# A conditional residual layer: the loads of SyncE's queue stand in line, and the first mask factors are split off

## The chip, the cores and the metric

One core of one Trainium2 chip. The metric is the device time of one execution, in microseconds (us); the lower the better. The kernel before took 590.72 us in the median of three runs (590.47 to 591.55).

## The reference

```python
x = x + _L0_cond_ref(x, cond_8, weight, mask, bias)       # x: 128 batches of 128 x 512

masked_w = weight * mask[None, :, :]                      # 8 groups of 512 outputs x 512 inputs
w_bot = jnp.einsum('bg,got->bot', y, masked_w)            # y = cond_8, 128 x 8
return jnp.einsum('bnt,bot->bno', x, w_bot) + bias
```

For each batch b, eight weight matrices are mixed with the eight numbers of y, the mixture is masked, and the batch's 128 x 512 tile of x is multiplied by it; bias and x itself are added. All in fp32.

## The kernel before, in words

The outputs are cut into two slices of 256, the batches into four windows of 32: eight units, slice by slice. A unit has 16 groups of two batches. A unit's mixed weights are made in 16 bursts of TensorE matmuls, each on 16 outputs (L567, `burst`), which land in PSUM as four tiles of a bank each. Two of the four are brought into `wbot` by VectorE, multiplied by the mask on the way (L469, with `factor_sb`), two by ScalarE as plain copies (L388); for these the mask was put on the weights beforehand, by VectorE for the first pair of chunks and by GpSimd for the others (L284, `multiply_mask`, which waits for the load of the weights and for the load of the mask). The weights `wm` of slice 0 are loaded at the start and those of slice 1 during the fourth unit, over those that are done with.

The jobs are the matmuls of x against the mixed weights. In unit 0 the first eight groups are done in halves as the weights arrive. In the others most groups are done whole (L594, `piece`), one after another, and the rest in rounds of four jobs (L613, `turn`) between which the next unit's bursts are put: such a stage takes four turns. The eight PSUM banks are shared by bursts and jobs in the order in which they come free (`share_banks`), so a burst or a turn can wait for an eviction on VectorE.

The output tile `staged` has six buffers of 512 columns. For output tile m SyncE loads x into it (`load_xn`, L334), VectorE adds the bias (L490), then the sums (L503, from PSUM or from the copy `late_sb` that ScalarE makes), and ScalarE's queue stores it (L393). VectorE's work is in program order: while it waits in L490 for a load of `xn`, the evictions behind it wait too. In a stage of whole groups the bias of tile m+1 is added right after the sums of tile m; in a stage of turns the biases stand between the evictions of the bursts.

SyncE issues nearly all loads, in the order of its program: at the start the weights and masks of a pair of chunks, two of x, one of xn, and so on; then, for each group n from 10 on, the xn that are due (up to four tiles ahead), and x of group n (512 KB, L326) into the buffer of group n-10, for which it waits until that group's last job is done. In the fourth unit, behind eight of these groups, stand a load of weights (512 KB) and one of mask (256 KB), and one of factors (512 KB): that is slice 1. Nothing limits how many loads are under way at once, but the buffers: a load waits when its buffer is in use. ScalarE's queue issues the first mask, y, the first half of the factors, the bias and all stores.

Of the kernel before, what the change touches and what calls it, by code (L numbers as in the profile page):

```python
# [34 lines left out]
OUTB = 6  # L35
# [82 lines left out]
ENDING = JOBS_OF[OUT_TILES - 1]  # L118

X_LEAD = 4  # L120


BANK_OF, TAKEN_FROM = {}, {}
# [74 lines left out]
def cond_resid_kernel(nc: bass.Bass, x, xn, w, mask, factor, bias, yblk, out):  # L198
# [5 lines left out]
    with ctx:  # L204
# [3 lines left out]
        def sem(name):  # L208
            return ctx.enter_context(nc.semaphore(name))
# [23 lines left out]
        s_w = [sem(f"s_w{i}") for i in range(CS)]  # L233
        s_mask = [sem(f"s_mask{i}") for i in range(PAIRS)]
        s_factor = [sem(f"s_factor{i}") for i in range(2)]
        s_mul_v = sem("s_mul_v")
        s_mul_p = sem("s_mul_p")
        s_x = [sem(f"s_x{i}") for i in range(XRING)]
# [63 lines left out]
        def stored(eng, m):  # L302

            eng.wait_ge(s_out[m % OUTB], 16 * (m // OUTB + 1))

        @block.sync
        def _(eng):
            def load_blocks(s, at, count):
                eng.dma_start(wm[:, at:at + count, :], w[s, :, at:at + count, :]).then_inc(s_w[at], 16)  # L309

            def load_mask(s, q):
                eng.dma_start(mask_sb[:, :] if s else first_mask[:, q, :], mask[s, q]).then_inc(s_mask[q], 16)  # L312

            def load_factor(s, half):
                at = slice(half * HALF, (half + 1) * HALF) if s == 0 else slice(0, CS)
                eng.dma_start(factor_sb[:, at, :], factor[s, :, at, :]).then_inc(s_factor[half], 16)  # L316

            def load_x(n):
                if n >= XRING:
                    eng.wait_ge(s_s2, LAST_JOB[X_ORDER[n - XRING]] + 1)  # L320
                elif n >= XRING - PAIRS // GB:
                    q = (n - XRING) * GB + PAIRS
                    masked(eng, 0, q)
                    masked(eng, 0, q + 1)
                u, g = X_ORDER[n]
                eng.dma_start(xs[:, n % XRING, :, :, :], x[u % WINDOWS * GROUPS + g]).then_inc(s_x[n % XRING], 16)  # L326

            def load_xn(m):

                if m == 0:  # L330
                    eng.wait_ge(s_s1, 1)
                elif m >= OUTB:
                    stored(eng, m - OUTB)
                eng.dma_start(staged_of(m), xn[m]).then_inc(s_xn[m % OUTB], 16)  # L334

            load_blocks(0, 0, 1)
            load_blocks(0, 1, 1)
            for q in range(1, PAIRS // 2):
                load_mask(0, q)
                load_blocks(0, 2 * q, 1)  # L340
                load_blocks(0, 2 * q + 1, 1)
            load_x(0)
            load_x(1)
            load_xn(0)
            n = 2
            for q in range(PAIRS // 2, PAIRS):
                load_mask(0, q)
                load_blocks(0, 2 * q, 2)
                if q == PAIRS // 2:
                    load_factor(0, 1)  # L350
                for n in range(n, n + (2 if q < PAIRS - 2 else 1)):
                    load_x(n)
                n += 1
                load_xn(q - PAIRS // 2 + 1)
            load_x(n)
            load_xn(OUTB - 1)
            load_x(n + 1)
            ahead = OUTB
            for n in range(XRING, STEPS):

                end = TILE_OF[LAST_JOB[X_ORDER[n - XRING]]] + X_LEAD + 1
                for m in range(ahead, end):
                    load_xn(m)
                ahead = max(ahead, end)
                load_x(n)
                if n in LOAD_W_AT:
                    q = LOAD_W_AT[n]
                    eng.wait_ge(s_s1, ((WINDOWS - 1) * CS + 2 * q + 2) * TILES)
                    load_blocks(1, 2 * q, 2)
                    if q:  # L370
                        masked(eng, 1, q - 1)
                    load_mask(1, q)
                if n == LOAD_FACTOR_AT:
                    b = WINDOWS * CS - 1
                    for j in range(TILES):
                        if on_vector(b, j):
                            tile_evicted(eng, b, j, GROUPS)
                    load_factor(1, 0)
            for m in range(ahead, OUT_TILES):
                load_xn(m)  # L380

        @block.scalar
        def _(eng):
            def evict(behind):
                for b, j, first, end in parts_of(behind):
                    if not on_vector(b, j):
                        tile_ready(eng, b, j)
                        eng.activation(tile_place(b, j, first, end), tile_sums(b, j, first, end),  # L388
                                       ACT.Copy).then_inc(s_ev_a, 1)

            def store_out(m):
                eng.wait_ge(s_o, JOBS_BY[m])
                eng.dma_start(out[m], staged_of(m)).then_inc(s_out[m % OUTB], 16)  # L393

            def load_y(u):
                if u >= 2:
                    eng.wait_ge(s_s1, (u - 1) * CS * TILES)
                eng.dma_start(y_sb[:, u % 2, :], yblk[u % WINDOWS]).then_inc(s_y[u % 2], 16)

            def store_last():  # L400
                for i in ENDING:
                    eng.wait_ge(s_o, i + 1)
                    at = STARTS[i] % BANK
                    eng.dma_start(out[OUT_TILES - 1, :, at:at + WIDTH[i]],
                                  staged_job(i)).then_inc(s_out[(OUT_TILES - 1) % OUTB], 16)

            eng.dma_start(first_mask[:, 0, :], mask[0, 0]).then_inc(s_mask[0], 16)  # L407
            load_y(0)
            eng.dma_start(factor_sb[:, 0:HALF, :], factor[0, :, 0:HALF, :]).then_inc(s_factor[0], 16)
            for b in range(HALF):  # L410
                evict(b)
                if b == HALF - 4:
                    eng.dma_start(bias_sb[:, :], bass.AP(tensor=bias.tensor, offset=bias.offset,
                                                         ap=[[0, P], [1, NO]])).then_inc(s_bias, 16)
            kept = made = 0

            def store_made():
                for m in range(kept, made):
                    store_out(m)
                return made  # L420

            def take_out(jobs):
                for i in jobs:
                    if i in LATE[2:]:
                        eng.wait_ge(s_o, LATE[LATE.index(i) - 2] + 1)
                    eng.wait_ge(s_s2, i + 1)
                    eng.activation(late_of(i), ps[BANK_OF[i, None]][:, 0:SL], ACT.Copy).then_inc(s_late, 1)  # L427

            for stage in STAGES:
                if stage.jobs[0] in NEXT_Y:  # L430
                    load_y(NEXT_Y[stage.jobs[0]])
                if stage.around:
                    for n in range(TILES + 1):
                        if n == TILES:
                            take_out(stage.jobs[2:])
                        for b in stage.bursts_at(n):
                            evict(b)
                            kept = store_made()
                else:
                    for b in stage.bursts:  # L440
                        evict(b)
                        kept = store_made()
                if made - kept >= 2:
                    kept = store_made()
                end = stage.jobs[-1]
                made = min((STARTS[end] + WIDTH[end]) // BANK, OUT_TILES - 1)
            kept = store_made()
            store_last()
            for i in range(OUTB):
                count = len(range(i, OUT_TILES, OUTB)) + (len(ENDING) - 1 if i == (OUT_TILES - 1) % OUTB else 0)  # L450
                eng.wait_ge(s_out[i], 16 * count)
# [8 lines left out]
        def _(eng):  # L460
            def evict(behind):
                for b, j, first, end in parts_of(behind):
                    if on_vector(b, j):
                        tile_ready(eng, b, j)
                        if b in (0, HALF):
                            eng.wait_ge(s_factor[b // HALF], 16)  # L466
                        elif b == WINDOWS * CS:
                            eng.wait_ge(s_factor[0], 32)
                        eng.tensor_tensor(tile_place(b, j, first, end), tile_sums(b, j, first, end),  # L469
                                          factor_of(b, j, end - first), ALU.mult).then_inc(s_ev_v, 1)  # L470
# [228 lines left out]
```

## Time and profile before

| | us |
|---|---|
| median of three runs | 590.72 (590.47 to 591.55) |
| the profiled execution, its own time | 591.91 |
| its span, first to last instruction | 589.9 |
| DVE busy | 337.4 (57%) |
| ACT busy | 159.5 (27%) |
| POOL busy | 20.0 (3%) |
| DMA | 149.96 MB, mean 254 GB/s |

Start with the busy shares: the engine with nearly the whole span is the bound, and of the others only their waits matter. Then read where the busy engine stands still, from the chain of waits (the work that ended last, followed back), and ask of each wait which transfer ended it. The slices of DMA traffic show where the 16 DMA engines are full: they are from the start to about 44 us and again around 255 to 285 us.

### The profile page before, as it was taken

How to read it: one execution, taken by the hardware profiler on the slowest of the kernel's cores; microseconds unless marked ns; L12 is line 12 of the kernel's file. 1: busy time of each engine (PE TensorE's matmuls, PEld its weight loads, DVE VectorE, ACT ScalarE, POOL GpSimd, SP SyncE). 2: the span in 40 equal slices, each digit the busy share in tenths (PEclk: the TensorE clock that was granted, in tenths of full speed). 3: DMA queues.
4: the chain of work that ended last, by engine and by line, in shares of the span. 5: the costliest groups of instructions: out<-in, count | busy, mean ns of one | idle time of the engine just before them, and what ended most of it. 6: DMA issues, size and time to landing. Idle time of an engine off the chain costs nothing.

```text
span 589.9 us, 20560 instructions
## 1 busy us (share of the span) xinstructions
PE 578.9 (98%) x9084; PEld 544.1 (92%) x9084; DVE 337.4 (57%) x616; ACT 159.5 (27%) x332; POOL 20.0 (3%) x19
## 2 busy tenths in 40 slices
PE   8899999999999999999999999999999999999998
PEld 6799999989998999889999899998999989999887
DVE  5673667436673466734766356763567535665343
ACT  4340445004440144301443023420334203441000
POOL 2110000000000011001000000000000000000000
PEclk9999999999999999999999999999999999999999
DMA  8998656895579868799686975779566794758942
GB/s 315 400 349 311 212 195 208 299 313 181 195 227 305 288 204 275 246 340 410 240 277 229 336 234 176 240 227 334 177 218 216 239 343 173 233 168 291 310 146 89
DMA packets 62583, 149.96 MB, mean 254 GB/s; under 512 B 6944, under 2 KB 8352, under 8 KB 62496
## 3 DMA queue, kind: packets, MB, share of 16 engines
q1 hardware_dynamic: 42192, 113.79, 58.1%
q10 hardware_dynamic: 20304, 34.87, 15.7%
q8 instruction: 71, 1.16, 0.8%
q14 instruction: 16, 0.13, 0.1%
HBM read 115.08 MB, written 33.55 MB: 252 GB/s over the span
## 4 chain that ended last, share of the span: by engine, by line
PE 95%; DMA 3%; issue 1%; SPq 0%; DVE 0%; ACTq 0%; DVEq 0%
PE ps L594 42%; PE ps L613 34%; PE ps L567 19%; DMA staged<-in_xn 2%; DMA y_sb<-in_yblk 1%; DVE staged L503 0%; SPq L326 0%; SPq L312 0%; SPq L316 0%; SPq L309 0%; ACTq L407 0%; SPq L334 0%; DVEq L466 0%; DVE staged L490 0%; DVEq L501 0%
## 5 line engine op out<-in xcount | busy, mean ns | idle before, releaser
L594 PE MATMUL ps<-wbot,xs 128*128 128x256 f32 (+1 forms) x1400 | 253.7, 343 | 0.7 <-ACT wbot L388 0.7
L594 PEld LDWEIGHTS ps<-wbot,xs 128*128 128x128 f32 x1400 | 227.1, 191 | 25.3 <-issue 0.9
L388 ACT ACTIVATE wbot<-ps 128x512 f32<-128x512 f32 (+2 forms) x275 | 139.8, 566 | 347.0 <-PE ps L567 346.5
L613 PE MATMUL ps<-wbot,xs 32*128 32x256 f32 x3584 | 220.4, 376 | 1.2 <-issue 1.1
L469 DVE TENSOR_TENSOR wbot<-ps,factor_sb 128x512 f32<-128x512 f32 (+2 forms) x276 | 165.4, 646 | 85.5 <-PE ps L567 84.3
L613 PEld LDWEIGHTS ps<-wbot,xs 32*128 32x128 f32 x3584 | 187.3, 185 | 3.8 <-issue 2.4
L503 DVE TENSOR_TENSOR staged<-ps,staged 128x256 f32<-128x256 f32 (+2 forms) x145 | 73.6, 523 | 158.4 <-PE ps L594 140.3
L567 PEld LDWEIGHTS ps<-y_sb,wm 32*128 32x128 f32 x4096 | 147.2, 188 | 11.6 <-issue 6.7
L567 PE MATMUL ps<-y_sb,wm 32*128 32x128 f32 x4096 | 149.9, 276 | 5.2 <-issue 3.8
L490 DVE TENSOR_TENSOR staged<-staged,bias_sb 128x512 f32<-128x512 f32 (+2 forms) x137 | 89.1, 655 | 2.2 <-DMA staged<-in_xn 2.2
L427 ACT ACTIVATE late_sb<-ps 128x256 f32<-128x256 f32 x56 | 18.6, 381 | 24.4 <-PE ps L613 24.4
L503 DVE TENSOR_TENSOR staged<-late_sb,staged 128x256 f32<-128x256 f32 x56 | 21.8, 430 | 0.0
L284 POOL TENSOR_TENSOR wm<-wm,mask_sb 128x512 f32<-128x512 f32 x8 | 10.9, 1366 | 254.7 <-DMA mask_sb<-in_mask 254.7
L284 POOL TENSOR_TENSOR wm<-wm,xs 128x512 f32<-128x512 f32 x7 | 8.9, 1273 | 28.1 <-DMA wm<-in_w 28.1
L621 PE MATMUL ps<-staged 128*128 128x512 f32 x4 | 3.8, 1101 | 1.4 <-DVE staged L505 1.4
L621 PEld LDWEIGHTS ps<-staged 128*128 128x128 f32 x4 | 1.2, 326 | 2.5 <-DVE staged L505 1.4
L284 DVE TENSOR_TENSOR wm<-wm,xs 128x512 f32<-128x512 f32 x1 | 0.7, 692 | 3.5 <-DMA xs<-in_mask 3.5
L388 ACT ACT_TABLE_LOAD x1 | 1.3, 1283 | 2.1 <-issue 2.1
L505 DVE MEMSET staged<- 128x512 f32 x1 | 0.5, 485 | 0.9 <-PEq L647 0.9
L647 POOL MEMSET const-float32-0.0<- 128x1 f32 x1 | 0.1, 98 | 0.2 <-issue 0.2
L647 POOL MEMSET const-bfloat16-1.0<- 128x1 bf16 x1 | 0.1, 101 | 0.0
L647 POOL MEMSET const-uint8-127<- 128x1 uint8 x1 | 0.1, 101 | 0.0
(1 smaller groups left out, 0.1 us busy)
## 6 DMA issues: line engine op xcount, KB each, us to landing
xs<-in_x SPq DMA_DIRECT2D x128, 512.0 KB, 5.4
staged<-in_xn SPq DMA_DIRECT2D x128, 256.0 KB, 4.2
out<-staged ACTq DMA_DIRECT2D x127, 256.0 KB, 5.3
wm<-in_w SPq DMA_DIRECT2D x12, 512.0 KB, 8.3
wm<-in_w SPq DMA_DIRECT2D x8, 256.0 KB, 6.4
mask_sb<-in_mask SPq DMA_DIRECT2D x8, 256.0 KB, 6.2
xs<-in_mask SPq DMA_DIRECT2D x7, 256.0 KB, 9.7
y_sb<-in_yblk ACTq DMA_DIRECT2D x8, 64.0 KB, 5.3
```

Of the source, the lines that this page charges most:

```text
L284: return eng.tensor_tensor(wm[:, 2 * q, :], wm[:, 2 * q, :], by, ALU.mult)
L388: eng.activation(tile_place(b, j, first, end), tile_sums(b, j, first, end), ACT.Copy).then_inc(s_ev_a, 1)
L427: eng.activation(late_of(i), ps[BANK_OF[i, None]][:, 0:SL], ACT.Copy).then_inc(s_late, 1)
L469: eng.tensor_tensor(tile_place(b, j, first, end), tile_sums(b, j, first, end), factor_of(b, j, end - first), ALU.mult).then_inc(s_ev_v, 1)
L490: ins = eng.tensor_tensor(at, at, bias_of(i, at.shape[1]), ALU.add)
L503: eng.tensor_tensor(at, total, at, ALU.add).then_inc(s_o, 1)
L505: eng.memset(staged[:, 0, :], 0.0).then_inc(s_zeros, 1)
L567: ins = eng.matmul(bank[:, k * P:(k + 1) * P], wm[rows, block_of(c, j), k * P:(k + 1) * P], y_sb[rows, u % 2, :], start=True, stop=True)
L594: ins = eng.matmul(bank[:, at:at + width], group[:, h, k, :], sums_of(slice(0, P), u, g, h, c, end, k), start=(k == 0), stop=(k == KT - 1))
L613: ins = eng.matmul(ps[BANK_OF[i, None]][:, 0:WIDTH[i]], xs[rows, X_AT[u, g] % XRING, h, k, :], sums_of(rows, u, g, h, c, end, k), start=(n ...
L621: eng.matmul(ps[BANKS - 1][:, :], staged[:, 0, 0:P], staged[:, 0, :], start=True, stop=True)
L647: nc = bacc.Bacc("TRN2", target_bir_lowering=False, num_devices=1, dynamic_dma_scratch_size=64)
```

## The change

SyncE keeps a list of the loads that it has sent. Before it sends one, it waits until the last but one of the list has landed (so two are under way at most); in the opening (slice 0's weights and masks, the first ten x, the first six xn) until the last but three has landed (four under way). The second half of slice 0's factors follows the rule of two. Nothing is reordered on SyncE, and all former waits stay. On ScalarE's queue, the load of the factors of chunks 0 to 7 (256 KB) becomes two: chunks 0 and 1 (64 KB), then 2 to 7 (192 KB), with a semaphore each, and VectorE waits for the first before burst 0's eviction, for the second before burst 2's.

```diff
+FIRST_LINE, LINE = 4, 2
...
+        s_factor_soon = sem("s_factor_soon")
...
+            sent = []
+
+            def stand_in_line(most, landing, times):
+
+                if len(sent) >= most:
+                    before, landings = sent[-most]
+                    eng.wait_ge(before, 16 * landings)
+                sent.append((landing, times))
+
             def load_blocks(s, at, count):
+                stand_in_line(LINE if s else FIRST_LINE, s_w[at], s + 1)
                 eng.dma_start(wm[:, at:at + count, :], w[s, :, at:at + count, :]).then_inc(s_w[at], 16)
 
             def load_mask(s, q):
+                stand_in_line(LINE if s else FIRST_LINE, s_mask[q], s + 1)
...
             def load_factor(s, half):
                 at = slice(half * HALF, (half + 1) * HALF) if s == 0 else slice(0, CS)
+                stand_in_line(LINE, s_factor[half], s + 1)
...
                 u, g = X_ORDER[n]
+                stand_in_line(LINE if n >= XRING else FIRST_LINE, s_x[n % XRING], n // XRING + 1)
...
+                stand_in_line(LINE if m >= OUTB else FIRST_LINE, s_xn[m % OUTB], m // OUTB + 1)
                 eng.dma_start(staged_of(m), xn[m]).then_inc(s_xn[m % OUTB], 16)
...
-            eng.dma_start(factor_sb[:, 0:HALF, :], factor[0, :, 0:HALF, :]).then_inc(s_factor[0], 16)
+            eng.dma_start(factor_sb[:, 0:2, :], factor[0, :, 0:2, :]).then_inc(s_factor_soon, 16)
+            eng.dma_start(factor_sb[:, 2:HALF, :], factor[0, :, 2:HALF, :]).then_inc(s_factor[0], 16)
...
-                        if b in (0, HALF):
-                            eng.wait_ge(s_factor[b // HALF], 16)
+                        if b == 0:
+                            eng.wait_ge(s_factor_soon, 16)
+                        elif b == 2:
+                            eng.wait_ge(s_factor[0], 16)
+                        elif b == HALF:
+                            eng.wait_ge(s_factor[1], 16)
```

## Rows read from the trace of the kernel before

**Rows 1.** Busy time; then from the waits, TensorE's for "issue": us, times, longest.
```profile
PE 578.9 (98%) x9084; PEld 544.1 (92%) x9084; DVE 337.4 (57%) x616; ACT 159.5 (27%) x332; POOL 20.0 (3%) x19
...
PE ps L567 <- issue: 3.8, 4, 1.3
...
PE ps L613 <- issue: 1.1, 2, 0.6
```

**Rows 2.** The chain of waits, 0 to 30 us: start, us, what.
```profile
10.64 13.18 DMA staged<-in_xn
...
24.45 0.43 DVE staged L503
...
24.93 1.15 PE ps L567 x26
```

**Rows 3.** DMA traffic, 0 to 44 us, in 40 slices.
```profile
GB/s 0 47 220 398 384 292 307 376 406 412 404 408 404 391 391 404 402 404 402 387 404 410 412 391 400 393 413 400 412 404 402 404 413 396 358 284 376 369 255 129
```

**Rows 4.** Timeline, 0 to 40 us: start, us, instruction, in brackets the idle before it.
```profile
7.99 1.29 DVE L469 TENSOR_TENSOR wbot<-ps,factor_sb 128x512 f32<-128x512 f32 x2 [2.45 <-PE ps L567]
...
23.84 0.69 DVE L490 TENSOR_TENSOR staged<-staged,bias_sb 128x512 f32<-128x512 f32 x1 [1.75 <-DMA staged<-in_xn]
```

**Rows 5.** Issues in windows with one load, 148.5 and 160.0 us: KB, us to landing.
```profile
staged<-in_xn SPq DMA_DIRECT2D x1, 256.0 KB, 2.6
...
xs<-in_x SPq DMA_DIRECT2D x1, 512.0 KB, 3.6
```

**Rows 6.** DMA issues, 107 to 130 us.
```profile
xs<-in_x SPq DMA_DIRECT2D x7, 512.0 KB, 4.6
staged<-in_xn SPq DMA_DIRECT2D x8, 256.0 KB, 4.2
```

**Rows 7.** DMA issues, 255 to 283 us.
```profile
xs<-in_x SPq DMA_DIRECT2D x8, 512.0 KB, 9.1
staged<-in_xn SPq DMA_DIRECT2D x9, 256.0 KB, 6.8
```

**Rows 8.** Stages: busy us of PE, PEld, DVE, ACT, POOL (instructions); clock, DMA share, GB/s.
```profile
106.00:130.00 24.00, 24.00 (x116) 20.85 (x114) 8.09 (x13) 0.00 (x0) 0.00 (x0) 1.00 0.94 317
130.00:170.00 40.00, 40.00 (x955) 39.78 (x958) 27.62 (x49) 17.09 (x34) 0.00 (x0) 1.00 0.60 197
254.70:286.00 31.30, 31.30 (x368) 28.59 (x370) 14.65 (x25) 5.00 (x10) 2.97 (x3) 1.00 0.95 363
```

**Rows 9.** Timeline of DVE, 254 to 300 us.
```profile
268.26 0.68 DVE L490 TENSOR_TENSOR staged<-staged,bias_sb 128x512 f32<-128x512 f32 x1
271.10 0.69 DVE L503 TENSOR_TENSOR staged<-ps,staged 128x512 f32<-128x512 f32 x1 [2.16 <-PE ps L594]
...
282.10 0.68 DVE L490 TENSOR_TENSOR staged<-staged,bias_sb 128x512 f32<-128x512 f32 x1
283.43 1.29 DVE L469 TENSOR_TENSOR wbot<-ps,factor_sb 128x512 f32<-128x512 f32 x2 [0.65 <-PE ps L567]
285.26 0.76 DVE L503 TENSOR_TENSOR staged<-ps,staged 128x256 f32<-128x256 f32 x2 [0.54 <-PE ps L613]
...
294.84 0.76 DVE L503 TENSOR_TENSOR staged<-ps,staged 128x256 f32<-128x256 f32 x2 [0.45 <-PE ps L613]
```

**Rows 10.** Timeline of PE, 312 to 318 us.
```profile
315.36 2.35 PE L567 MATMUL ps<-y_sb,wm 32*128 32x128 f32 x64
```

**Rows 11.** Timeline of PE in the fourth unit's preparation: two waits.
```profile
229.24 0.61 PE L567 MATMUL ps<-y_sb,wm 32*128 32x128 f32 x12 [0.78 <-issue]
...
241.62 0.61 PE L567 MATMUL ps<-y_sb,wm 32*128 32x128 f32 x12 [1.32 <-issue]
```

**Rows 12.** Stores issued at 24.9 and at 44.1 us, KB, us to landing.
```profile
out<-staged ACTq DMA_DIRECT2D x1, 256.0 KB, 7.4
...
out<-staged ACTq DMA_DIRECT2D x1, 256.0 KB, 2.0
```

**Rows 13.** DMA issues in a window that holds the loads issued at 254.7 us.
```profile
staged<-in_xn SPq DMA_DIRECT2D x1, 256.0 KB, 3.2
```

## The prediction

> **What bounds the kernel now.** I read the busy shares first: TensorE works 578.9 of a 589.9 us span [rows 1], and its granted clock stands at full in every stage that I looked at [rows 8]. So there is little to win anywhere but in its idle time, and much to lose wherever a load comes late. Next, the chain of waits at the start [rows 2]. Until 24.93 us TensorE hangs on transfers: the chain runs through one load of xn, issued at 10.64 and landed 13.18 us later, at 23.82. VectorE had waited 1.75 us for it [rows 4], adds the bias, then the sums at 24.45, and that frees the bank with which TensorE goes on. From there TensorE has no wait that is worth a name but those put down to "issue": with the opening's they make 3.8 and 1.1 us over the span [rows 1]. The third view is the DMA traffic: near 400 GB/s from 3 to about 37 us [rows 3], so SyncE's loads of the opening queue up behind each other, and a load issued early lands no earlier for it. Then the later stages: 0.60 of the DMA engines' time in a stretch of turns, 0.94 in one of whole groups, and 0.95 from 254.7 to 286, where slice 1's weights are added [rows 8].
>
> **The factor split.** VectorE's first eviction started at 7.99 after an idle time that TensorE ended, not the factors [rows 4]. An earlier landing of the first 64 KB frees nothing, and the other 192 KB are wanted only by burst 2, about 1.6 us later. One more issue on ScalarE's queue stands ahead of its first copy, which also waits for TensorE. Cost 0. Bounds: 0.2 us either way, a third of a 256 KB load's 0.65 us share of a full queue, for how its bytes fall among the others.
>
> **The line of four in the opening.** The order stays, and the bound is bytes. A 256 KB load takes 256 KB / 0.4 per ns = about 0.66 us of the full queue, four of them 2.6 us. With four under way, one is sent when the fourth before it lands, and lands itself a round trip later. The shortest round trip of such a load is 2.6 us [rows 5]: just enough to keep the queue full, with no margin. In the busy opening a round trip can only be longer, so about seven loads of 256 KB go a little slower, perhaps 0.03 to 0.05 us each; once x (512 KB, 1.3 us of the queue each) is among the four there is margin. The one load under the rule of two, the factors' second half, leaves a gap of 0.1 to 0.2 us. All lies ahead of the xn that ends at 23.82, and what is lost there is lost to TensorE one for one. I take 0.3 us; bounds -0.2 (nothing lost, and the split's gain) and +1.2 (the busy loads at 3.2 us a round trip [rows 13]: 0.6/4 us for each of eight). TensorE's other waits ahead of 24.93 give nothing back, whatever becomes of them: it waits for that xn anyway.
>
> **The line of two from then on.** This is the large item. Two loads under way mean that each costs half a round trip. The quiet round trips are 3.6 us for x and 2.6 for xn [rows 5], together 3.1 us for a pair at the best; where loads and stores crowd, 4.6 and 4.2 [rows 6], or 4.4 us a pair. A whole group takes TensorE 3.45 us and asks for one such pair and one store (VectorE's sums follow each other at that distance; 271.10 is one [rows 9]). So in whole groups the line is about as fast as the demand or slower, and in turns (two pairs in 9.6 us, from 285.26 to 294.84 [rows 9]) it has time to catch up. x is fetched ten groups ahead, so a lag of a few us there costs nothing. xn is up to four tiles ahead; that covers a few us as well, but not where slice 1's loads come in between.
>
> There I count. The xn issued at 254.7 lands 3.2 us later [rows 13], at 257.9. Behind it in SyncE's program stand 15 loads up to and with the xn whose bias is added at 282.10 [rows 9]: eight of 512 KB (five x, two of weights, the factors) and seven of 256 KB (five xn, two masks). In the traces' state that xn lands before it is needed, since all are queued at once, at 6.8 to 9.1 us a load [rows 7]. In the line of two I take 3.8 and 3.0 us, near the quiet rows, since at most one load stands ahead of each, with 0.2 to 0.4 us for the stores: 8 x 1.9 + 7 x 1.5 = 25.7 us, and some 0.6 for where two 512 KB loads follow each other. It lands at 284.2, 2.1 us after it is wanted. Earlier, the xn wanted at 268.26 is the seventh load: 257.9 + 4 x 1.9 + 3 x 1.5 = 270.0. It is late by 1.7, but VectorE has nothing to do until the sums at 271.10 [rows 9], less 0.68 for the bias: free. At 282.10 it isn't: the two evictions of 283.43 (1.29 us) stand behind it and would end at 284.2 + 0.7 + 1.3 = 286.2, while the next turn, which takes their banks, starts at about 285.3. That is 0.9 us of TensorE idle; with 0.3 for the next biases of the stage, 1.2 us. The last mask of slice 1 is 15 loads further, eight and seven again: 284.2 + 25.7 = 309.9, masked by 311.3, and its burst runs at 315.36 [rows 10]. That holds. Bounds: with 3.6 and 2.6, 23.5 us, and the xn of 282.10 lands at 281.4: cost 0. With 4.6 and 4.2, 33.1 us: it lands at 291, 9 us late; as TensorE's own delay puts off the demand, and VectorE can give 1.2 of it, I count the stretch at 7 us at most.
>
> **TensorE's issue waits.** The two largest outside the opening, 0.78 and 1.32 us [rows 11], fall where slice 1's loads crowd the queue, and no instruction of another engine ends them. What ends them the rows don't show. I take no change; bounds -2.1 (both go) and +1.0.
>
> There is one row that makes such a gain thinkable: a store landed in 7.4 us behind SyncE's long queue and in 2.0 us beside an empty one [rows 12], so a transfer on another queue does feel SyncE's depth. The Trainium skill, "DMA: Bandwidth & Descriptors", section "Queues, rings and completion order", says that each DMA engine goes round robin between the queues that have work and takes a packet from each. By that rule depth would not matter as long as one load is always under way, and the gain would be 0; the row of 7.4 us speaks against it.
>
> The same page ("Anatomy of one DMA") gives 2.0 us and bytes / 436 GB/s for a transfer: 3.2 and 2.6 us, an estimate by which a pair costs 2.9 us, below the 3.45 of a group, and the line of two would cost nothing. The trace agrees on the quiet 256 KB load (2.6) and is higher on the other (3.6) [rows 5].
>
> **The sum.** 0 + 0.3 + 1.2 + 0 = +1.5 us against the profiled execution's own 591.91 us (span 589.9, and 2.0 around it). That execution lay 1.2 us above the median of the runs, 590.72; the same steps on the median give 592.2 us.
>
> **The rivals.**
> *Hidden anyway* (chance 0.27): the round trips stay at the quiet rows, the lag of 254 to 285 us stays inside the lead of xn. Only the opening's 0.2 us are left: 590.9 us. For it: the quiet rows, and the rest of the unit in turns. Against: stores run beside every load there.
> *Faster* (0.17): the shorter queue lets other queues' transfers through sooner, and TensorE's two issue waits of slice 1's loads go; with the opening's 0.2, 590.7 + 0.2 - 2.1 = 588.8 us. It decides only if the xn of 282.10 comes in time, under 24.2 us for the 15 loads. For it: [rows 11, 12]. Against: no row ties those waits to a transfer.
> *The line is too slow* (0.13): round trips of about 4.3 and 3.8 us, 30.5 us for the 15 loads, so 6.9 us late at 282.10 less the 1.2 that VectorE can give: 5.7, and 0.6 in the opening: 597.0 us. For it: [rows 6]. Against: those loads had others in front.
> *The split does what it is named for* is part of these: it would show VectorE's first eviction waiting for factors before, and it doesn't.
>
> **How the numbers follow.** The forecast (0.43) has its own range of 591.3 to 594.0. No change from slower can be told by measurement below 0.2%, 1.2 us. Slower by more (above 591.9): the third rival, and three quarters of the forecast's 0.43: 0.46. Faster: 0.17. Within: 0.27 and the rest of the forecast's: 0.37. The range of 8 in 10 goes from 589.2, which leaves out half of the faster rival, to 595.8, which leaves out most of the too slow one.
>
> **What would show it.** In the changed kernel's profile: SyncE waits for its own landings; x and xn land in 3 to 4.5 us everywhere, and never in 9; the xn that ends the opening's chain lands at 23.9 to 24.5; the bias near 282 waits for its load, and TensorE has an idle time at about 285 with VectorE's name on it. VectorE's first eviction starts at 8.0 as before. I am wrong if no L490 of the stretch waits (hidden), if the last mask reaches GpSimd after 314, or if TensorE's issue waits fall from 4.9 us in sum to under 3.

## The result, and the profile after

The changed kernel took 616.93 us in the median of four runs (612.5 to 620.69), the kernel before 591.13 beside it; the ratio is 1.0428, 95% interval 1.0384 to 1.0472. Ratios here and below are of executions in the faster of the program's two states; two of e14's twelve were in the slower one. The forecast was 592.2 us, the range 589.2 to 595.8. The direction was right; the size was not, and the time lies far outside the range.

The profiled execution has a span of 617.6 us against 589.9, 27.7 us more. Busy shares, then the clock by slice, of the changed kernel:

```profile
PE 584.6 (95%) x9084; PEld 547.2 (89%) x9084; DVE 338.3 (55%) x616; ACT 159.4 (26%) x332; POOL 19.2 (3%) x19
...
PEclk9899999999999999996898999999999999999999
```

TensorE is busy 5.7 us more than in [rows 1] with the same 9084 matmuls, and its granted clock dips in two places (a slice is 15.4 us). The rest, 22 us, is idle time. The opening first: chain of waits, 0 to 60 us (start, us, what), the answer to [rows 2].

```profile
1.64 4.88 DMA xs<-in_mask
6.53 3.53 DMA wm<-in_w
10.08 4.12 DMA wm<-in_w
14.22 6.91 DMA xs<-in_mask
...
22.46 5.50 DMA staged<-in_xn
...
28.59 0.43 DVE staged L524
...
29.06 2.07 PE ps L588 x26
```

Before, the chain had one load in it that waited in a full queue; now it goes from landing to issue to landing. The xn that frees TensorE lands at 27.96, not 23.82, and TensorE goes on at 29.06, not 24.93. The traffic of the first 44 us, the answer to [rows 3], has holes:

```profile
GB/s 0 32 236 383 362 365 399 304 292 298 246 266 214 324 363 333 343 169 322 82 196 296 343 384 397 307 346 335 287 350 399 330 359 348 300 369 239 288 311 366
```

The second place is slice 1's. The chain of waits from 268 to 300 us, part of a stretch from 234 to 374 in which it holds hardly anything but loads:

```profile
269.66 3.55 DMA xs<-in_x
...
273.28 4.32 DMA xs<-in_x
...
277.66 4.20 DMA staged<-in_xn
...
281.92 5.11 DMA wm<-in_w
...
287.09 2.67 DMA staged<-in_xn
```

The biases there, the answer to [rows 9] (timeline of DVE; in brackets the idle time before, and who ended it):

```profile
270.87 0.69 DVE L511 TENSOR_TENSOR staged<-staged,bias_sb 128x512 f32<-128x512 f32 x1 [7.43 <-DMA staged<-in_xn]
...
281.88 0.69 DVE L511 TENSOR_TENSOR staged<-staged,bias_sb 128x512 f32<-128x512 f32 x1 [5.42 <-DMA staged<-in_xn]
...
289.79 0.69 DVE L511 TENSOR_TENSOR staged<-staged,bias_sb 128x512 f32<-128x512 f32 x1 [6.49 <-DMA staged<-in_xn]
```

Behind each stand the sums, and with them the PSUM banks that TensorE waits for. Its first wait ends with the sums behind the bias of 289.79, its second with those behind the next bias, at 293.95 (timeline of PE, 276 to 300 us):

```profile
291.26 1.22 PE L634 MATMUL ps<-wbot,xs 32*128 32x256 f32 x4 [12.61 <-DVE staged L524]
295.42 3.35 PE L634 MATMUL ps<-wbot,xs 32*128 32x256 f32 x25 [2.94 <-DVE staged L524]
```

And the loads of 255 to 283 us, the answer to [rows 7]: short round trips, but few loads.

```profile
xs<-in_x SPq DMA_DIRECT2D x5, 512.0 KB, 3.6
staged<-in_xn SPq DMA_DIRECT2D x5, 256.0 KB, 3.4
```

The loads of x and xn are ten here and seventeen before; all queues together moved 6.84 MB in these 28 us against 10.84.

### The profile page after: what moved, and what is told of

It is laid out like the page before. It is cut to its first block, busy times and chain, and to the rows that moved or that the text cites. A ratio compares the mean times of both kernels' runs of the same rounds, so it can differ in the third digit from the quotient of the medians.

```text
span 617.6 us, 20819 instructions
## 1 busy us (share of the span) xinstructions
PE 584.6 (95%) x9084; PEld 547.2 (89%) x9084; DVE 338.3 (55%) x616; ACT 159.4 (26%) x332; POOL 19.2 (3%) x19
## 3 DMA queue, kind: packets, MB, share of 16 engines
q10 hardware_dynamic: 20448, 34.87, 15.4%
## 4 chain that ended last, share of the span: by engine, by line
PE 73%; DMA 25%; DVE 1%; issue 1%; SPq 0%; DVEq 0%
PE ps L615 31%; PE ps L634 27%; PE ps L588 15%; DMA staged<-in_xn 12%; DMA xs<-in_x 5%; DMA wm<-in_w 4%; DMA xs<-in_mask 2%; DMA mask_sb<-in_mask 2%; DVE staged L524 0%; DVE wbot L490 0%; SPq L341 0%; SPq L321 0%; DVE staged L511 0%; SPq L316 0%; SPq L330 0%
## 5 line engine op out<-in xcount | busy, mean ns | idle before, releaser
L615 PE MATMUL ps<-wbot,xs 128*128 128x256 f32 (+1 forms) x1400 | 254.7, 344 | 1.0 <-DVE wbot L490 1.0
L634 PE MATMUL ps<-wbot,xs 32*128 32x256 f32 x3584 | 227.9, 380 | 17.2 <-DVE staged L524 16.9
L634 PEld LDWEIGHTS ps<-wbot,xs 32*128 32x128 f32 x3584 | 192.3, 187 | 21.9 <-DVE staged L524 18.5
L588 PEld LDWEIGHTS ps<-y_sb,wm 32*128 32x128 f32 x4096 | 148.5, 188 | 17.8 <-POOL wm L286 5.3
```

Source lines behind the costliest of these rows:

```text
L588: ins = eng.matmul(bank[:, k * P:(k + 1) * P], wm[rows, block_of(c, j), k * P:(k + 1) * P], y_sb[rows, u % 2, :], start=True, stop=True)
L615: ins = eng.matmul(bank[:, at:at + width], group[:, h, k, :], sums_of(slice(0, P), u, g, h, c, end, k), start=(k == 0), stop=(k == KT - 1))
L634: ins = eng.matmul(ps[BANK_OF[i, None]][:, 0:WIDTH[i]], xs[rows, X_AT[u, g] % XRING, h, k, :], sums_of(rows, u, g, h, c, end, k), start=(n ...
```

## The experiments

Times are medians beside runs of the kernel before on the same chip. Lines are numbered by the kernel in question.

**e1_opening_only, e2_later_only.** The two halves of the line.

```diff
-                if len(sent) >= most:
+                if most and len(sent) >= most:
...
-FIRST_LINE, LINE = 4, 2
+FIRST_LINE, LINE = 4, 0      # e1 (the factors' second half keeps 2)
+FIRST_LINE, LINE = 0, 2      # e2
```

> The opening's line alone (four under way; the factors' second half, two), with the split; no line from the eleventh x and the seventh xn on. Theory A (a busy round trip of about 4 us, so a 256 KB load costs 1.0 us where the full queue gave 0.66; the xn that frees TensorE lands 4 us later, as at 27.96 in the changed kernel, and later work gives 1 to 2 us back): 595 to 597 us against 591.1. Rival B (the opening's loss is caught up by the leads, all of the 26 us comes from the later line): 591 to 592. Rival C (the opening's delay is what sets off the later one): near 617.

> The line of two from the eleventh x on, none in the opening. Theory A (each later load costs half a busy round trip of 4.2 us; from 211 us on, where slice 1's loads come in between, xn falls behind): 611 us, 608 to 614. Rival C (the lag is set off by the late opening): under 600. The two losses of e1 and e2 should add up to the changed kernel's 26 us if they are independent.

e1: 597.15 us, ratio 1.0123 (1.0081 to 1.0166). e2: 607.58 us, ratio 1.0292 (1.0237 to 1.0348). Theory A's account stands in both, though e1 lies 0.15 us above its range (595 to 597) and e2 0.4 below (608 to 614); e1's loss is not caught up by the leads (B falls), and e2 is far from under 600 (C falls). In e1's profile TensorE waits 4.1 us at 29.18 for VectorE's sums. The medians had seemed to leave 4.5 us over (5.4 and 15.9 make 21.3, the change lost 25.8); the ratios add up to 1.0415, inside the change's interval.

**e3_line3_later.** `FIRST_LINE, LINE = 0, 3`.

> No line in the opening, three under way later. Theory A (a third of a round trip per load, 4.6 us or so: 3.1 us a pair, under the 3.45 us of a group): 591 to 594 us. Rival D (it is the waits as such, SyncE's issue after a landing, whatever the number): 600 or more, half of e2's loss at least.

591.34 us, ratio 0.9988 (0.9953 to 1.0022). Three under way cost nothing that can be measured: D falls, it is the number. The profile still shows one wait of TensorE of 1.6 us, at 273.31, so three is near the edge.

**e4_split_only.** `FIRST_LINE, LINE = 0, 0`, the split kept.

> Only the factor split, no line anywhere. All theories: 591.1 within 1 us, since the first eviction waits for TensorE and not for factors. If the split had a price of its own (one more issue on ScalarE's queue, smaller packets), 592 or more.

590.34 us, ratio 0.9987 (0.9961 to 1.0014): the split does nothing that the time shows. VectorE's first eviction waits for TensorE as in [rows 4] and for the factors only in one trace, that of e15 (below), which has no split. Timeline of DVE, the changed kernel, then e15:

```profile
7.17 2.48 DVE L490 TENSOR_TENSOR wbot<-ps,factor_sb 128x512 f32<-128x512 f32 x4 [1.49 <-PE ps L588]
```
```profile
7.81 1.29 DVE L485 TENSOR_TENSOR wbot<-ps,factor_sb 128x512 f32<-128x512 f32 x2 [1.73 <-DMA factor_sb<-in_factor]
```

In both the 64 matmuls of the first burst took 2.07 us; in the kernel before they took 3.80, with the granted clock at 1.00 in all three; why they differ isn't known. In e15 TensorE's part was ready at 7.47, the undivided factors landed at 7.72, and the eviction started at 7.81: the split can save 0.3 us there, and it doesn't reach the total.

**e7_stretch_only, e8_all_but_stretch.** Where the later line costs.

```diff
+            now = [0]
...
             for n in range(XRING, STEPS):
+                now[0] = 2 if 50 <= n < 72 else 0     # e7
+                now[0] = 0 if 50 <= n < 72 else 2     # e8
```

> The line of two only for the loads between x 50 and x 71 (the stretch in which slice 1's weights, masks and factors are loaded), none elsewhere. Theory A (the lag builds up where slice 1's 17 loads come on top of a pair per group): nearly all of e2's 16 us, 602 to 608. Rival E (the lag builds up over the whole run): a fifth of it, 593 to 596.

> The complement: the line of two later on, but none between x 50 and x 71. Theory A: the leads of x and xn take the lag of the whole groups, 591 to 594. Rival E: 603 or more.

e7: 607.44 us, ratio 1.0287 (1.0215 to 1.0358), all of e2's loss. e8: 588.9 us, ratio 0.9955 (0.992 to 0.999), a gain that neither A nor E had. E falls.

**e9_small_stores.** e2 with stores of a sixteenth; the rest of the output is left out.

```diff
-                eng.dma_start(out[m], staged_of(m)).then_inc(s_out[m % OUTB], 16)
+                eng.dma_start(out[m, :, 0:32], staged_of(m)[:, 0:32]).then_inc(s_out[m % OUTB], 16)
```

> As e2, but each store writes 32 of its 512 columns (the rest of the output is left out), so a load's round trip has next to no stores beside it. Theory A with stores (the round trip of 4.2 us is 3.5 of its own and 0.7 from the store that goes beside it): 15 loads of the stretch take 26 us and not 31, so the loss falls from 16 us to between 1 and 6: 592 to 597. Rival F (the pair's own round trip is what is too long, stores don't matter): 604 or more.

592.53 us, ratio 1.0017 (0.9991 to 1.0043). F falls. The time isn't free of a loss in the stretch: TensorE still waits 1.93 and 2.60 us there for VectorE's sums, and the line's gain elsewhere (e8) stands against it. The loads of the 15-load stretch, first e2 (262 to 292.6 us), then e9 (259 to 285):

```profile
xs<-in_x SPq DMA_DIRECT2D x6, 512.0 KB, 3.7
staged<-in_xn SPq DMA_DIRECT2D x5, 256.0 KB, 3.4
out<-staged ACTq DMA_DIRECT2D x4, 256.0 KB, 4.0
wm<-in_w SPq DMA_DIRECT2D x2, 512.0 KB, 4.3
```
```profile
xs<-in_x SPq DMA_DIRECT2D x5, 512.0 KB, 3.6
staged<-in_xn SPq DMA_DIRECT2D x5, 256.0 KB, 2.8
wm<-in_w SPq DMA_DIRECT2D x2, 512.0 KB, 4.1
```

From issues and landings in the traces, for the same 15 loads each time (behind the xn that was issued at 254.7 before, up to the xn whose bias stood at 282.10), and what the number under way makes of the mean trip. The last column runs from the landing of that first xn to that of the last:

| kernel | under way | mean trip, us | 15 x trip / number | 15 loads took, us |
|---|---|---|---|---|
| e2 | 2 | 3.86 | 28.9 | 29.9 |
| the change | 2 | 4.10 | 30.7 | 30.9 |
| e9, small stores | 2 | 3.45 | 25.9 | 26.4 |
| e3 | 3 | 5.34 | 26.7 | 26.4 |
| e13 (below) | 4 | 5.35 | 20.1 | 19.5 |
| before | buffers alone | 7.96 | | 19.25 |

The last two columns agree within 4%: the line was full throughout, and the rate is the number under way over the round trip. With two it is under what the full queue gives, and the stores' share of a trip is 0.4 us (e2) to 0.65 (the change), somewhat less than the 0.7 that I had expected.

**e6_opening8, e11_opening6.** `FIRST_LINE, LINE = 8, 0` and `6, 0`, the factors' second half alike.

> Opening line of eight instead of four (the factors' second half too), none later. Theory A (eight loads of 256 KB are 5.3 us of the full queue, more than a busy round trip of 4): the xn that frees TensorE lands at 24 again, 591 within 1 us. Rival D (the wait as such costs): 593 or more.

> Opening line of six (the factors' second half too), none later. With four under way a 256 KB load's round trip was 3.8 us, 0.95 us a load; with eight 7.2, 0.9 a load at most and set by the full queue. Theory A (four are too few by about a half, six cover 4.0 us of the full queue): the xn that frees TensorE lands at 24 to 25.5, 591 to 593.5 us. Rival H (the loss is in proportion to the line, so between four and eight): 594 to 595.

Eight: 592.16 us, ratio 1.0002 (0.9968 to 1.0035). Six: 592.87 us, ratio 1.0007 (0.998 to 1.0034). The bias that waits for the xn of the opening's chain, in e1 (four), then in e11 (six):

```profile
28.09 0.69 DVE L511 TENSOR_TENSOR staged<-staged,bias_sb 128x512 f32<-128x512 f32 x1 [6.42 <-DMA staged<-in_xn]
```
```profile
24.59 0.69 DVE L511 TENSOR_TENSOR staged<-staged,bias_sb 128x512 f32<-128x512 f32 x1 [3.84 <-DMA staged<-in_xn]
```

Six is already enough, so H falls: not in proportion, but a threshold. Where between four and six it lies isn't shown, and these two kernels also lift the factors' second half from two to six or eight, so not all of the difference to e1 is that of the four. The round trips of six loads of 256 KB, first in the changed kernel (4.6 to 10 us), then in e6 (3 to 6 us):

```profile
wm<-in_w SPq DMA_DIRECT2D x4, 256.0 KB, 3.8
xs<-in_mask SPq DMA_DIRECT2D x2, 256.0 KB, 3.8
```
```profile
wm<-in_w SPq DMA_DIRECT2D x4, 256.0 KB, 7.2
xs<-in_mask SPq DMA_DIRECT2D x2, 256.0 KB, 7.2
```

3.8 us over four is 0.95 us a load, where the full queue landed one in 0.66.

**e10_opening_and_outer.** Opening of four, outer line of two, none between x 50 and 71.

> The changed kernel with no line between x 50 and x 71; the opening's four and the outer line of two stay. e1's 5.4 us and e2's 15.9 add up to 21, the changed kernel's loss is 26. Theory A (the 5 us of interaction arise in the stretch: the late opening leaves less lead when it begins): about e1, 595 to 598 us. Rival G (a late opening and the line of two cost together even without slice 1's loads, since two under way never catch up): 600 or more.

594.98 us, ratio 1.0038 (1.0013 to 1.0063): just below theory A's range, as the outer line's gain is in it. G falls.

**e12_outer_no_split, e13_outer2_stretch4.** The gain of e8, followed up; e13 has `now[0] = 4 if 50 <= n < 72 else 2`.

> The kernel before with the line of two outside the opening and outside x 50 to 71, no split. e8, which is this with the split, came out at a ratio of 0.9955. If the gain is the line's (stores and other queues' transfers land sooner): 589 us, ratio 0.993 to 0.998. If it was chance or the split's: 0.998 to 1.002.

> The line of two outside, of four between x 50 and x 71, split as in the change. Theory A (four under way: the stretch's 15 loads take about 20 us as without a line, since four trips of 5.3 us are the full queue's rate): like e8, 589 to 591 us. If four are too few there as in the opening: 594 or more.

e12: 589.51 us, ratio 0.9942 (0.9911 to 0.9973). e13: 588.43 us, ratio 0.992 (0.9892 to 0.9948), the best version here, ahead of both kernels. The gain is the line's, and four under way are enough where loads are large. (The intervals of e12 and e13 overlap, so which of the two is faster isn't settled.) Chain of waits of the kernel before, the pieces with which the units' whole groups begin (start, us, what), then the same of e13:

```profile
102.07 27.94 PE ps L594 x144
172.74 27.94 PE ps L594 x144
246.50 27.94 PE ps L594 x144
317.71 27.94 PE ps L594 x144
388.38 27.94 PE ps L594 x144
459.93 27.94 PE ps L594 x144
531.80 55.64 PE ps L594 x280
```
```profile
103.92 27.94 PE ps L617 x144
174.60 27.94 PE ps L617 x144
245.60 27.94 PE ps L617 x144
318.40 27.94 PE ps L617 x144
389.39 27.94 PE ps L617 x144
460.07 27.94 PE ps L617 x144
530.75 55.64 PE ps L617 x280
```

From one row to the next is a unit. Where nothing holds it up it takes 70.67 or 70.68 us. Before, four of six took more (73.76, 71.21, 71.55 and 71.87 us: 5.7 over in sum); in e13 five of six are within 0.4 us of it and one is over by 2.1. The last two of the six, which have no loads of slice 1, can be compared in all traces. Under a line of two (nine kernels: e2, e8 to e10, e12 to e15, the change) all eighteen take 70.67 or 70.68. With none there, or with three (seven kernels: before, e1, e3, e4, e6, e7, e11), thirteen of fourteen take longer, up to 73.05, and the mean is 0.9 us over. Over five units that is 4.5 us, about the gain of e12 and e13 (by their ratios 3.4 and 4.7 us).

**e14_outer2_late4.** The line of two up to x 55, four from 56 to 71.

> The line of two everywhere but the opening (none) and x 56 to 71 (four). Up to x 55 slice 1's loads are three pairs only, and in e2 the unit that ends with x 47's successors took 70.7 us where the kernel before took 73.8. Theory A (the cost begins where the whole groups meet slice 1's loads, x 56 on; before that the line only takes TensorE's issue waits away): like e13 or better, 586 to 589 us. If the three pairs of loads from x 50 to 55 already begin the lag: 591 or more.

589.45 us, ratio 0.9975 (0.9945 to 1.0004): the median of all twelve is just above A's range (586 to 589), that of the ten behind the ratio, 588.62, in it, and the interval of the ratio is not clear of 1. In its trace SyncE is 7 us behind at x 54 and 12 at x 60 (from buffer free to issue); in e13 0 and 6. So the three pairs of loads from x 50 on begin the lag, and the leads take most of it: TensorE waits once more for VectorE's sums, 1.5 us.

**e15_lines_no_split.** Both lines, no split.

> The changed kernel without the factor split. If both lines together cost more than their sum because the opening's lateness is never caught up: 615 to 618 us, and the profile shows SyncE 5 us or more behind at x 34 (buffer free to issue). If it was the profiled execution's own: 611 to 613 and under 3 us behind at x 34. If the split had a part in the loss: under 611.

614.12 us, ratio 1.0396 (1.0362 to 1.0429), near e1 and e2 in sum. At x 34 SyncE is 4.0 us behind; 8.8 in the changed kernel's profiled execution, the slowest of its four. Between my two cases, then: the backlog under the line of two varies, and no interaction of the two lines can be told from their sum.

## Why the prediction was wrong

**The factor split, 0 us:** right (e4), but the eviction's start "at 8.0 as before" was not: it was 7.17, and [rows 4] had shown only the slower first burst.

**The line of four, 0.3 us, bound 1.2:** wrong, 1.2% (e1), 5 to 7 us. The main step that failed is "the shortest round trip of such a load is 2.6 us: just enough to keep the queue full", and then 0.03 to 0.05 us a load for a busy queue. Loads under way beside others took 3.8 us, not 2.6 to 3.2, so each load cost 0.95 us and not 0.7. The upper bound was built on the 3.2 us of a load with one store beside it; nothing in the rows bounded a queue that is kept at four. The nearest row was 4.2 [rows 6]: over four it gives 1.05 us a load, and (1.05 - 0.66) x 8 = 3.1 us; with the measured 0.95 it is 2.3. The xn came 4.1 us late. A second term was mis-sized too: the factors' second half under the rule of two, "a gap of 0.1 to 0.2 us". SyncE sent it only at 21.14, when the mask that was sent two loads before it had landed. The pair of weights between the two landed 2.6 us behind the kernel before (22.36 against 19.75), that half 3.9 (24.53 against 20.59): 1.3 us more. No run has four under way without that rule of two, so the two shares are read from landings and not tested.

**The line of two, 1.2 us, at most 7:** wrong, 2.9% (e2), 16 to 17 us. The mechanism and the stretch were right (e7, e8); four steps were not.
- The round trips of 3.8 and 3.0 us, "near the quiet rows": mean 3.43. Measured 3.86 to 4.10. The 15 loads took 29.9 to 30.9 us against 25.7 (26.3 with the allowance for neighbours of 512 KB). My value is what e9 measured with hardly a store (3.45, 26.4 us): I had allowed too little for them. It is the smaller loads that feel them: in the stretch the x took 3.7 us in the median, the xn 3.4 and the masks 3.8 with stores (e2), and 3.6, 2.8 and 2.9 with hardly any (e9), though x and xn stand in the same line in both.
- The start: I let the xn issued at 254.7 land on time. It landed at 262.8 in e2 and 275.0 in the changed kernel, for slice 1's first loads from x 50 on had already used up the lead (e14). The capacity of the line should have been set against the demand of the whole unit.
- The xn of 268.26, "free": it is the seventh of the fifteen loads, and TensorE's longest wait hangs on it, not on the xn of 282.10 that I priced. In e2 it landed at 277.14, its bias stood at 277.16, the sums behind it ended at 278.57, and TensorE went on at 278.63; the wait after that one ends with the sums behind the ninth load. By the prediction's own numbers the margin there was 0.4 us (270.0, where 270.4 was the last moment for the bias); with trips like mine and a start only 1.5 us late (259.4, not 257.9), e9 has 4.5 us of these waits.
- "VectorE can give 1.2" and "7 us at most": the cap had no row. In e2 the five biases of 255 to 283 wait 5.4, 2.4, 5.9, 5.6 and 2.0 us. The whole groups' last sums then come late, TensorE's turns wait 7.07 and 2.20 us for them, and then it goes on at a lower clock (below).

Of the signs, the late last mask came too: "after 314" was 325.1 in e2 and 337.5 in the changed kernel, where I had 309.9.

**The issue waits, 0:** wrong, and the sign that was named for it (under 3 us) came: none of PE's rows in the changed kernel's waits names "issue", against 4.9 us [rows 1]. That alone doesn't make the rival *Faster* right. The sum differs between traces without a later line (4.9 before, 1.7 in e4, 4.1 in e11); with a line throughout the later part it is 0 to 1.6, yet e12, which gains 0.6%, has 3.2. e12 and e13, which have the line without its loss, gain 0.6 and 0.8%, and the units are as even as shown above. That a store feels SyncE's depth (7.4 us and 2.0 [rows 12]) had been the sign of it. In e2's profile stores land in 4.0 us in the median, in the kernel before in 5.3. What TensorE waits for in these places was not tried by itself. All six of these waits in the kernel before end 2.3 to 2.5 us after a packet of 16 KB has started on q8, the queue that the profile calls "instruction", and there are only 71 such packets in the whole span; so the waits may be for instructions that are loaded late. That the line of two evens the units out is shown, by what path is not.

The Trainium skill ("DMA: Bandwidth & Descriptors", "Queues, rings and completion order") has each DMA engine take packets from the queues in turn. That depth then wouldn't matter was my inference, and the traces don't bear it out: in the kernel before, a store took 2.0 us in the median with no load of SyncE under way, 4.3 with two, 5.4 with three and 7.1 with five, but with eight (6.5) and twelve (7.4, one store) hardly more. Whether the engines take turns these runs don't show. The prediction's 2.0 us and bytes / 436 GB/s stand on that page ("Anatomy of one DMA") for transfers issued by GpSimd, which the prediction left out; with SyncE's busy trips of 3.9 us and more the estimate by them, that the line of two costs nothing, was wrong.

**The rivals:** *The line is too slow* named the right cause and row, and priced it at 597.0 for want of the clock, the start and the sums behind the earlier biases. Its trips of 4.3 and 3.8 us (30.5 us for the 15 loads) were within 2% of what was measured. It had a chance of 0.13 because the loads of [rows 6] "had others in front"; but two under way have stores beside them, and each other.

## What to carry to other kernels

A limit on the transfers under way turns a queue into a closed loop: its rate is the number under way over the round trip, and the trip to put in is one taken while the other queues are busy, not that of a lone transfer. Set this rate against the demand of the densest stage and of the whole period around it, with the lead at its start, and don't let the price end at the first wait: the work behind it, and the clock after it, are late too. Where the rate has room to spare a shorter queue can even gain, as it did here outside slice 1's loads (0.6 to 0.8%); why it does is open.

## What the runs showed that I had not expected

The clock after idle time. TensorE stood still for most of 270 to 278 us in e2 (timeline of PE, 276 to 284 us):

```profile
278.63 1.22 PE L634 MATMUL ps<-wbot,xs 32*128 32x256 f32 x4 [7.07 <-DVE staged L524]
282.05 2.52 PE L634 MATMUL ps<-wbot,xs 32*128 32x256 f32 x20 [2.20 <-DVE staged L524]
```

Windows of that kernel (busy us of PE, PEld, DVE, ACT, POOL; clock, DMA share, GB/s):

```profile
270.00:278.00 8.00, 1.56 (x35) 1.16 (x34) 2.19 (x4) 1.09 (x2) 1.26 (x1) 0.73 0.71 220
278.00:283.00 5.00, 2.17 (x12) 1.37 (x16) 2.96 (x5) 0.00 (x0) 0.00 (x0) 0.50 0.83 259
283.00:290.00 7.00, 7.00 (x123) 6.56 (x119) 2.08 (x4) 1.08 (x2) 0.00 (x0) 0.69 0.74 253
```

The granted clock is 0.50 from 278 to 283, the lower of its two levels (1.2 GHz), and it is back at full only in the course of the last window, in which TensorE was busy throughout. So 9.3 us of waiting there cost more than 9.3 us. In the opening of the changed kernel the same happened after TensorE's wait of 3.9 us: 0.50 from 29 to 33 us.

A round trip grows with what is under way: 3.9 us with two, 5.3 with three or four, 8.0 with the queue left alone. Three and four have the same trip but 26.4 and 19.5 us for the 15 loads: up to four the line sets the rate, and four reach what the free queue gave (19.25).
